# A twelve-sublayer model on one core: the deep sublayer's pipeline is put in a new order on all engines

## The reference, cut to what matters

```python
for i in range(DEPTH):          # 6
    x = attn_layer(shift_tokens(x), Wqkv[i], q_scale[i], k_scale[i], Wo[i]) + x
    x = ffn_layer(shift_tokens(x), ln_g[i], ln_b[i], W1[i], b1[i], W2[i], b2[i]) + x
```

## Time and profile before

| what | value |
|---|---|
| median of 3 runs | 5902.59 us |
| profiled execution, own time | 5911.22 us |
| its span | 5909.5 us |
| PE busy | 4787.8 us (81%) |
| PE weight loads busy | 2686.1 us (45%) |
| DVE busy | 3740.4 us (63%) |
| ACT busy | 2323.8 us (39%) |
| POOL busy | 3022.0 us (51%) |
| mean granted clock of PE | 0.864 of full speed |
| first deep call | 1519 to 3636 us |
| second deep call | 3786 to 5909 us |

### The profile page before, as it was taken

The page is one execution under the profiler, slowest core; times in us unless marked ns, Lnnn a source line. Parts: engine busy times, 40 slices in busy tenths (PEclk is TensorE's granted clock), DMA queues, the critical chain, the costliest instruction groups (busy, mean ns, idle before and its releaser), DMA issues.

```text
span 5909.5 us, 144803 instructions
## 1 busy us (share of the span) xinstructions
PE 4787.8 (81%) x64876; PEld 2686.1 (45%) x64876; DVE 3740.4 (63%) x4537; ACT 2323.8 (39%) x2527; POOL 3022.0 (51%) x1329
## 2 busy tenths in 40 slices
PE   6997699765688888888888886578888888888887
PEld 3443333332354555555455453245455455455554
DVE  5365366324477777777777674477677777777774
ACT  1241244341344444444444442244444444444443
POOL 0010000000577777777777660287677777777772
PEclk7697699766689998899999987589899989999998
DMA  2000000000010111111111111011111111111110
GB/s 62 1 1 0 0 1 1 0 0 0 30 29 21 47 25 25 41 26 44 25 44 25 26 25 45 0 28 26 25 44 25 45 25 44 25 37 30 28 25 22
DMA packets 78086, 144.29 MB, mean 24 GB/s; under 512 B 18728, under 2 KB 24944, under 8 KB 75824
## 3 DMA queue, kind: packets, MB, share of 16 engines
q1 hardware_dynamic: 77488, 135.23, 8.8%
HBM read 39.75 MB, written 1.05 MB: 7 GB/s over the span
## 4 chain that ended last, share of the span: by engine, by line
PE 52%; issue 21%; DVE 14%; ACT 7%; POOL 6%; DMA 0%; SPq 0%; DVEq 0%; POOLq 0%
PE psum L1028 12%; PE psum L1090 5%; PE psum L997 5%; PE psum L1078 5%; PE psum L1059 5%; DVE arena L1293 4%; ACT arena L1183 3%; PE psum L1011 3%; PE psum L1045 3%; DVE arena L1306 3%; DVE arena L1302 3%; POOL arena L1406 2%; PE psum L992 2%; PE psum L524 2%; POOL arena L1408 2%
## 5 line engine op out<-in xcount | busy, mean ns | idle before, releaser
L1406 POOL TENSOR_TENSOR arena<-arena,minus_half 128x16 f32<-128x16 f32 x384 | 1124.4, 2928 | 1039.0 <-DVE arena L1295 1036.8
L1411 POOL TENSOR_TENSOR arena<-arena 128x1024 f32<-128x1024 f32 x384 | 889.1, 2315 | 30.1
L1408 POOL TENSOR_TENSOR arena<-arena 128x1024 f32<-128x1024 f32 x384 | 902.9, 2351 | 0.0
L1183 ACT ACTIVATE arena<-psum 128x1024 f32<-128x1024 f32 x384 | 393.1, 1024 | 1043.1 <-PE psum L1028 1043.1
L1293 DVE TENSOR_REDUCE arena<-arena 128x16 f32<-128x1024 f32 x384 | 466.9, 1216 | 448.0 <-ACT arena L1183 446.4
L1028 PE MATMUL psum<-deep_wqkv,arena 128*128 128x512 f32 x768 | 456.6, 726 | 247.2 <-DVE arena L1306 239.3
L1028 PE MATMUL psum<-arena 128*128 128x512 f32 x768 | 424.5, 680 | 184.0 <-DVE arena L1306 184.0
L1045 PEld LDWEIGHTS psum<-w_ident,arena 128*128 128x128 f32 x3072 | 400.0, 152 | 253.8 <-issue 249.8
L1421 POOL MEMSET arena<- 128x33 f32 x4 | 0.4, 127 | 993.2 <-DVE std L1640 993.2
L1285 DVE TENSOR_TENSOR arena<-arena 128x1024 f32<-128x1024 f32 x192 | 491.6, 2560 | 6.6
L1302 DVE TENSOR_TENSOR arena<-psum,arena 128x1024 f32<-128x1024 f32 x384 | 467.6, 1218 | 0.0
(11 more groups left out here) (256 smaller groups left out, 7756.1 us busy)
## 6 DMA issues: line engine op xcount, KB each, us to landing
arena<-arena SPq DMA_DIRECT2D x672, 128.0 KB, 2.4
deep_wqkv<-in_deep_wqkv SPq DMA_DIRECT2D x6, 1536.0 KB, 7.0
arena<-in_deep_wqkv SPq DMA_DIRECT2D x6, 1536.0 KB, 6.8
arena<-arena SPq DMA_DIRECT2D x96, 64.0 KB, 2.0
deep_wo<-in_deep_wo SPq DMA_DIRECT2D x6, 512.0 KB, 7.4
arena<-in_deep_wo SPq DMA_DIRECT2D x6, 512.0 KB, 7.4
deep_w<-in_deep_w SPq DMA_DIRECT2D x6, 341.0 KB, 7.6
arena<-in_deep_w SPq DMA_DIRECT2D x6, 341.0 KB, 7.5
```

Source lines behind the costliest of these rows:

```text
L1183: nc.scalar.activation(qk_sq[:, HALVES[half], :], qk_half, ACT.Square).then_inc(de.deep_qk_squared, 1)
L1406: nc.gpsimd.tensor_tensor(h_inv[a % 2][:, hs], h_sum[a % 2][:, hs], minus_half[:, :], ALU.pow).then_inc(de.deep_inv_ready, 1)
L1408: nc.gpsimd.tensor_tensor(dst[:, hs, :], dst[:, hs, :], turned[:, hs, :], ALU.add).then_inc(de.deep_summed, 1)
L1411: nc.gpsimd.tensor_tensor(dst[:, hs, :], dst[:, hs, :], over(h_inv[a % 2][:, hs], [P, LHEADS, LD]), ALU.mult).then_inc(de.deep_roped, 1)
```

## The change

Every engine's list of a step is written in a new order. Scores and the value projection now belong to tile s - 2, the mix to tile s - 3. Softmax and division follow one another directly on DVE, with the exp between them on ACT. `rope_dve` is split: `parts_dve` (the two rotary products) now precedes `squares_dve` (sum and clamp), and POOL adds the products before it takes the power. The output product is split into three pairs (t = 2) and five (t = 3, one step later), mean and centring stand at the end of t = 3, variance and spread in t = 0, gates and two a products in t = 1, the third a product, hidden and down in t = 2, and the end of the unit at the head of t = 3. Down writes bank 7 instead of 6. The bank and data waits follow the new order. The lag of the last step is 11 instead of 12 steps behind the last unit's start. No operation is added or taken away. The core of the diff (new lists whole; the old ones are printed above):

```diff
-        LAST = 4 * (UNITS + 2)
+        LAST = 4 * (UNITS - 1) + 11
 # scores_pe
             if j >= 2:
                 pe.wait_ge(de.deep_o_kept, i - 1)
+            elif j == 1:
+                pe.wait_ge(de.deep_less_max, i)
 # probs_turn_pe
-            if s < ALL + 3:
-                pe.wait_ge(de.deep_v_kept, c * ALL + s - 2)
+            if j + 1 < ALL:
+                pe.wait_ge(de.deep_turn_kept, 2 * (i + 2))
 # turn_pe
-            if half == 1:
+            if half == 1 and a >= 1:
+                pe.wait_ge(de.deep_v_kept, i)
+            elif half == 1:
                 pe.wait_ge(de.deep_turn_kept, 2 * i + 1)
-            elif s >= 5:
-                pe.wait_ge(de.deep_probs_kept, c * ALL + s - 4)
+            elif a >= 2:
+                pe.wait_ge(de.deep_probs_kept, i - 1)
 # value_pe
-            if s - 1 < ALL:
-                pe.wait_ge(de.deep_turn_kept, 2 * (c * ALL + s))
+            if a + 1 < ALL:
+                pe.wait_ge(de.deep_turn_kept, 2 * i + 3)
...
+        WO_FIRST = 3
+        def wo_first_pe(pe, c, m):
+            g_ = c * UNITS + m
             pe.wait_ge(de.deep_o_kept, TILES * (g_ + 1))
             if m >= 1:
+                pe.wait_ge(de.deep_hidden_ready, 3 * (g_ - 1) + 2)
...
         def mean_pe(pe, c, m):
+            if m >= 1:
+                pe.wait_ge(de.deep_unit_end, g_)
...
         def deep_pe(pe, c):
+                ending, begun = 0 <= n - 2 < UNITS, 0 <= n - 1 < UNITS
+                # (each guarded by its range of s, as before)
+                qk_pe(pe, c, s, 0)
+                turn_pe(pe, c, s - 1, 0)
+                scores_pe(pe, c, s - 2)
+                if t == 0 and ending: var_pe(pe, c, n - 2)
+                if t == 1 and ending: gate_pe(.., 0); gate_pe(.., 1)
+                if t == 2 and ending: a_pe(pe, c, n - 2, 2)
+                if t == 3 and begun: wo_rest_pe(pe, c, n - 1)
+                value_pe(pe, c, s - 2)
+                qk_pe(pe, c, s, 1)
+                turn_pe(pe, c, s - 1, 1)
+                mix_pe(pe, c, s - 3)
+                if t == 1 and ending: gate_pe(.., 2); a_pe(.., 0)
+                if t == 2 and ending: down_pe(pe, c, n - 2)
+                if t == 3 and begun: mean_pe(pe, c, n - 1)
+                probs_turn_pe(pe, c, s - 2)
+                if t == 0 and ending: spread_pe(pe, c, n - 2)
+                if t == 1 and ending: a_pe(pe, c, n - 2, 1)
+                if t == 2 and begun: wo_first_pe(pe, c, n - 1)
         def deep_act(act, c):
+                probs_act(s - 3); [t == 0: ln_square_act(n - 2)]
+                square_act(s, 0); turn_act(s - 1, 0); [t == 1: affine_act(n - 2)]
+                exp_act(s - 2); value_act(s - 2)
+                [t == 1: gelu_act(n - 2, 0); gelu_act(n - 2, 1)]
+                square_act(s, 1); turn_act(s - 1, 1); o_act(s - 3)
+                [t == 1: gelu_act(n - 2, 2)]
         def deep_dve(dve, c):
+                [t == 1: scale_dve(n - 2)] [t == 2: hidden_dve(n - 2, 1)] [t == 3: end_dve(n - 2)]
+                parts_dve(s, 0); squares_dve(s, 0); softmax_dve(s - 2)
+                [t == 0: var_dve(n - 2)] [t == 2: hidden_dve(n - 2, 2)]
+                divide_dve(s - 2); [t == 3: attn_dve(n - 1)]
+                parts_dve(s, 1); squares_dve(s, 1)
+                [t == 1: hidden_dve(n - 2, 0)] [t == 2: shift_dve(n + 1)] [t == 3: centre_dve(n - 1)]
 # rope_pool: the sum L1408 now precedes the power L1406; rstd_pool stands between half 0 and half 1 of t == 0
```

More of the change, by code:

```diff
@@ L1086, in wo_pe, with wo_rest_pe @@
             if m >= 1:
-                pe.wait_ge(de.deep_unit_end, g_)
+                pe.wait_ge(de.deep_hidden_ready, 3 * (g_ - 1) + 2)
             wo = layer_of(m).wo
-            for pair in range(PAIRS):
-                last = nc.tensor.matmul(bank(6), wo[:, pair, :], oT[:, pair, :], start=(pair == 0), stop=(pair == PAIRS - 1))
+            for pair in range(WO_FIRST):
+                nc.tensor.matmul(bank(6), wo[:, pair, :], oT[:, pair, :], start=(pair == 0), stop=False)
+        def wo_rest_pe(pe, c, m):
+            wo = layer_of(m).wo
+            for pair in range(WO_FIRST, PAIRS):
+                last = nc.tensor.matmul(bank(6), wo[:, pair, :], oT[:, pair, :], start=False, stop=(pair == PAIRS - 1))
             last.then_inc(de.deep_attn_ready, 1)
         def mean_pe(pe, c, m):
-            pe.wait_ge(de.deep_ffn_shifted, 2 * (c * UNITS + m) + 2)
+            g_ = c * UNITS + m
+            if m >= 1:
+                pe.wait_ge(de.deep_unit_end, g_)
+            pe.wait_ge(de.deep_ffn_shifted, 2 * g_ + 2)
             nc.tensor.matmul(bank(7), w.avg[:, :], xf, start=True, stop=True).then_inc(de.deep_mean_ready, 1)
@@ L1132, in down_pe @@
             for j, (c0, rows) in enumerate(DIB):
-                last = nc.tensor.matmul(bank(6), layer_of(m).w2[0:rows, j, :], hidden[0:rows, j, :], start=(j == 0), stop=(j == 2))
+                last = nc.tensor.matmul(bank(7), layer_of(m).w2[0:rows, j, :], hidden[0:rows, j, :], start=(j == 0), stop=(j == 2))
             last.then_inc(de.deep_ffn_ready, 1)
@@ new lines, in deep_pe @@
+                if t == 1 and ending:
+                    gate_pe(pe, c, n - 2, 0)
+                    gate_pe(pe, c, n - 2, 1)
+                if t == 2 and ending:
+                    a_pe(pe, c, n - 2, 2)
+                if t == 3 and begun:
+                    wo_rest_pe(pe, c, n - 1)
+                if 0 <= s - 2 < ALL:
+                    value_pe(pe, c, s - 2)
+                if s < ALL:
+                    qk_pe(pe, c, s, 1)
+                if 0 <= s - 1 < ALL:
+                    turn_pe(pe, c, s - 1, 1)
@@ L1167, in deep_pe @@
[L1167 to L1174, removed]
+                if t == 2 and ending:
+                    down_pe(pe, c, n - 2)
+                if t == 3 and begun:
+                    mean_pe(pe, c, n - 1)
@@ L1178, in square_act @@
+                if 0 <= s - 2 < ALL:
+                    probs_turn_pe(pe, c, s - 2)
+                if t == 0 and ending:
+                    spread_pe(pe, c, n - 2)
+                if t == 1 and ending:
+                    a_pe(pe, c, n - 2, 1)
+                if t == 2 and begun:
+                    wo_first_pe(pe, c, n - 1)
         def square_act(act, c, a, half):
@@ L1260, in deep_act @@
                     turn_act(act, c, s - 1, 1)
[L1261 to L1264, removed]
+                if 0 <= s - 3 < ALL:
+                    o_act(act, c, s - 3)
+                if t == 1 and ending:
+                    gelu_act(act, c, n - 2, 2)
         def softmax_dve(dve, c, j):
@@ L1290, in rope_dve @@
             dve.wait_ge(de.deep_qk_squared, 2 * i + half + 1)
[L1291 to L1295, removed]
             if half == 0 and a // TILES % NB == 0:
@@ L1347, in end_dve @@
             dve.wait_ge(de.deep_ffn_ready, c * UNITS + m + 1)
-            nc.vector.scalar_tensor_tensor(zu, bank(6), layer_of(m).vec[:, 2:3], zu, ALU.add, ALU.add).then_inc(de.deep_unit_end, 1)
+            nc.vector.scalar_tensor_tensor(zu, bank(7), layer_of(m).vec[:, 2:3], zu, ALU.add, ALU.add).then_inc(de.deep_unit_end, 1)
         def shift_dve(dve, c, n):
```

139 lines of the change are left out of this document (65 added, 74 removed).

## The result

The change made the kernel slower. The median is 5936.32 us (4 runs, 5932.90 to 5949.42) against 5901.27 us of the kernel before in the same comparison (4 runs), a ratio of 1.0063 with a 95% interval of 1.0045 to 1.0080. I had forecast 5506, with 5360 to 5710 as the range and 0.06 for slower.

A forecast was written before the change was run, and what follows sets the result against it. Work order, not one full engine, was taken as the bound. Steps summing to 75.7 us plus 2.5 for the clock gave 78.2 a unit; with filling and drain, two calls saved 396 us: 5506, range 5360 to 5710.

The forecast's parts named there:

- reduce plus clamp 2521.07 - 2519.73 = 1.34: VectorE's square sum and clamp in each half: 1.34 us, placed behind the rotary products so the next projection needn't wait.
- D: Start of a step's first rotary product on VectorE; in the base step the next one comes 16.7 us later.
- near D + 4.5 behind the preceding half 1: GpSimd's start on half 0 in t = 0, after the preceding half 1; half 0 finished about D + 12.6.
- rival 2: Division's product at 1.22 us beside only GpSimd's power, no half-clock cost: unit 73.9 us, total 5318; chance 0.12.
- about 4: Upper bound in us for the division's product: a blocked GpSimd operation of 2.91 plus its own 1.22; 2.5 was taken.
- +2.5 us a unit: TensorE's clock cost: about two half-clock stretches a unit whose delay of 1.1 to 1.7 us reaches the end.
- 0 and +14.4: Bounds in us a unit for TensorE's clock cost; the upper has all eight projections at half clock.
- rival 1: TensorE's 2.15 us gaps halve its clock nearly each time: unit 81.7 us, total 5660; chance 0.22.
- The slower rival: Projection always starts at half clock after TensorE waits for VectorE: unit 90.1 us, total 6050; chance 0.06.
- The full-clock walk: The four steps of a unit summed at full clock: 75.7 us against 84.8 before.
- The exp is bare by 1.1 us: Between softmax and division on VectorE, the exp is no longer covered by a rotary half: loss of 1.1 us per step.
- The spread's wait of 5.28 us: TensorE's idle before spread, waiting for rstd from GpSimd: to fall from 5.28 us to under 1.5.

The follow-up runs named there:

- e6: The kernel before, with only rotary products put ahead of square sum and clamp on VectorE, and add ahead of power on GpSimd: 5841.33 us against 5904.39.
- e5: The changed kernel with unread products put on TensorE behind the second projection, four in t = 0 and three in t = 2: 5594.35 us.
- e9: The changed kernel with the clamp done by GpSimd and nothing else changed: 5388.89 us, ratio 0.9130 to the kernel before.
- e2: The changed kernel with VectorE's clamp of the square sums left out, GpSimd waiting for the sums instead: 5364.24 us.
- e3: The changed kernel with square sums and clamp again ahead of the rotary products, and GpSimd's power ahead of its add: 5562.31 us.
- e4: The changed kernel with the clamp on GpSimd and the value copy ahead of the exp in t = 0, 1, 2: 5293.91 us.

## Why the prediction was wrong

**The step that failed** is the term "reduce plus clamp 2521.07 - 2519.73 = 1.34", carried unchanged into a new place. Before, POOL mostly had nothing to do until the clamp was done, and the clamp took 175 ns in the median. The new order puts it behind the products, and the second product also releases POOL's add. There it takes 1380 ns on average, and reduce plus clamp about 2.6 us (3.40 in the step above). Of the 384 clamps 371 began under POOL's add and ended 0.03 to 0.04 us behind its end. My walk couldn't see this for half 0, since it let the clamp end at D + 3.6 and POOL start "near D + 4.5 behind the preceding half 1". In the step above D is 2529.35 and the add began at 2532.73, D + 3.4, ahead of the clamp. On average it began at D + 2.4 to 2.9: POOL was waiting for DVE there, 1218.4 us over the whole run (before L1427), and was not behind.

I had the rule in hand: the Trainium skill, "SBUF — State Buffer", section "SBUF: two separate sides", says that VectorE in a two-port mode (it then uses the port pair shared with GpSimd too), or with two inputs in SBUF against a GpSimd operation that reads SBUF, and GpSimd keep one another out for a whole instruction. The trace agrees with it for the clamp beside the add, to 0.03 us in the step above (2535.10 and 2535.07); no view shows the clamp's mode. I applied it only to the division's product, and not to each DVE operation that the change moves beside POOL. The old trace showed it for small and one-input operations too: the longest clamp there took 674 ns beside POOL's scaling, and the shifted copy of the earlier trace rows 1.29 us, which POOL idle brings to 0.42. POOL's power did not shut DVE out, although it reads SBUF; here the measurement decides against the rule. The division's product began under the power for `rstd` in 44 of 192 cases and took 1.22 each time, and in e6 a clamp inside the long power took 0.17:

```profile
2540.10 1.01 POOL L1437 TENSOR_TENSOR rstd<-arena,minus_half 128x4 f32<-128x4 f32 x1
2540.16 1.22 DVE L1299 TENSOR_TENSOR arena<-arena 128x1024 f32<-128x1024 f32 x1
```

```profile
1559.28 2.91 POOL L1408 TENSOR_TENSOR arena<-arena,minus_half 128x16 f32<-128x16 f32 x1
1560.63 0.17 DVE L1307 TENSOR_SCALAR arena<-arena 128x16 f32<-128x16 f32 x1
```

(The first two rows are of the changed kernel, the last two of e6.) So the product did fall to 1.22, as my rival 2 had it; that rival missed the other side of the exchange. The bound of "about 4" for it, with the power as what blocks, had no ground.

**The second size that was off** is the clock, +2.5 us a unit within "0 and +14.4". The mechanism was named: PE idle from D + 6.0 to 8.15, waiting for the value copy. With the clamp behind the add, the exp began at D + 7.2 to 7.7 on average instead of 6.1, and in t = 0 PE was done at D + 5.3 instead of 6.0. The wait came to 4.6 us on average in t = 0, 1.8 in t = 1, where I had none, and 3.1 in t = 2. Filling it (e5) gave back 7.8 of the 87.1 us, so the clock's price on the path was at least that. This followed from the first step: with the short clamp (e9) the waits were 1.6, 0.6 and 1.5 us and the unit 75.4, so there +2.5 would have been too much. My rival 1 saw this mechanism at 81.7; it was still too small by 5.4, because it didn't have the clamp under it. The slower rival (projection always at half clock) is not what happened: of these steps' 332 projections two were over 2.4 us, and the turn and the mix ran slow.

**What held.** The full-clock walk gave 75.7 a unit with a short clamp; e2, which is that case, measured 74.8 and e9 75.4. The exp is bare by 1.1 us, as said (DVE's wait before the division's reduction, L1295 of the changed kernel, was 0.95 on average and 1.1 at most). The spread's wait of 5.28 us left, as said: over the whole run PE waited for POOL there 4 times, 5.5 us in all. t = 3 came to 18.4 against 19.2: the shifted copy took 0.42 with POOL idle, not 1.29. The drain was about 67 us against 57 predicted and 95 before. What did not hold: t = 2 fell only to 25.4 and stayed the longest step, above the 23 that I had named as a sign of being wrong; the call's clock of 0.86 stayed just above its mark, 0.85. And my gains by step compared distances of scores groups before with distances of D after. By projection starts on both sides the forecast was +1.7, -1.8, -8.5 and -0.8 us for t = 0 to 3; the sum is hardly touched by this. The call before stands at 2114 us in the forecast, where the earlier trace rows have 2117; that is 6 us over both calls.

**How the loss divides.** With the value copy first, the blocked clamp costs 75.9 - 73.1 = 2.8 us a unit. With the clamp off DVE, the late value copy costs 75.4 - 73.1 = 2.3. Together they cost 87.1 - 73.1 = 14.0. The remaining 8.9 exist only when both are there, and e5's 7.8 suggest that most of it is the clock's. In the kernel as changed, where the value copy is late, the clamp alone is therefore worth 87.1 - 75.4 = 11.7 a unit, 547 us in all (5936.32 - 5388.89). That is more than the 430 by which I missed, since the rest of the forecast was too high by 117 us for the kernel with a short clamp (5506 against e9's 5389). That part of the miss worked in my favour by luck.

**What stays open.** I didn't measure how the clock's answer depends on the wait's length; e3, with waits of at most 2.5 us, stood at 0.95, between the others. In a t = 1 step of the changed kernel the mix ran slow after a wait of only 1.95 us, and in e9 23 of 42 mixes of t = 0 were over 2.5 us behind waits of 1.6 us on average, so no length shown here is safe. Nor did I split e3's gain among its other parts.

## What to carry to other kernels

When an edit moves a VectorE instruction, price it anew beside what GpSimd does at that moment; here even 16 elements a partition waited for the end of a GpSimd add of 2.35 us. In an in-order list, look for an instruction whose input is ready but which stands behind one that waits, above all if TensorE hangs on it. Delays on the way to TensorE need not add: here each of two cost 2.3 to 2.8 us a unit alone and 14.0 together, much of it (at least 7.8, by e5) through the clock, so a test that removes one of two causes can seem to explain everything.

## What the runs showed of the hardware that was not expected

- A 128x16 f32 TENSOR_SCALAR on DVE took 174 to 177 ns with POOL idle (358 of 384 in the kernel before) and up to 2345 ns beside POOL's 128x1024 add: the 371 that began under the add in the changed kernel ended 0.03 to 0.04 us behind its end. Moved to POOL, the same clamp took 272 ns (e4).
- POOL's powers held neither that clamp (0.17 us inside one of 2.91) nor a DVE product with both inputs in SBUF (1.22 us across one of 1.01).
- The granted clock over the same stretch went from 0.87 to 0.98 when unread products filled two of a unit's three waits, and the kernel got 5.8% faster by them.
